# A three-stage attention kernel on one core: one masked score tile moved from TensorE to VectorE, new slot plans for its stages, and 64 extra products where two stages begin

## What is computed

```python
def stage0(q, k, mask):             # 8 heads of 16 channels, 256 positions, grouped conv (3 taps)
    qh, kh, vh = gconv(q, wq), gconv(k, wk), gconv(v, wv)
    att = softmax(qh.T @ kh / sqrt(8) - 1e9 * mask)
    return layernorm(att @ vh + q.T)
def stage1(x, mask):                # 16 heads of depth 16, 128 positions, mask shared by all
    return layernorm(x + mha(x, x, x, mask))
def stage2(x, ctx, padding):        # keys and values from ctx, a padding mask for each sequence
    return layernorm(x + mha(ctx, ctx, x, padding))
def ffn(x):
    return layernorm(x + relu(x @ w1 + b1) @ w2 + b2)
```

## Time and profile before

| | |
|---|---|
| median of 3 runs | 4481.46 us (4481.1 to 4481.8) |
| the profiled execution: its time, its span | 4476.52 us, 4474.7 us |
| PE, DVE, ACT, POOL busy, share of the span | 93%, 79%, 70%, 64% |
| mean granted TensorE clock | 0.985 |
| first stage, second, third, feed-forward begin at about | 0, 1612, 2705, 3724 us |

### The profile page before, as it was taken

One profiled execution on the slowest core, in us unless ns is written; L12 is line 12 of the kernel. 1 busy time (PEld: TensorE's weight loads), 2 busy tenths in 40 slices (PEclk: granted clock), 3 DMA queues, 4 the chain that ended last, 5 costly groups with the idle time before them and its releaser, 6 DMA issues. The chain is left out here.

```text
span 4474.7 us, 129562 instructions
## 1 busy us (share of the span) xinstructions
PE 4144.4 (93%) x46216; PEld 3376.6 (75%) x46216; DVE 3523.3 (79%) x13839; ACT 3136.7 (70%) x6279; POOL 2872.4 (64%) x4568
## 2 busy tenths in 40 slices
PE   7999999999999969999999986999999997999999
PEld 5777777777777747777777765788787776999998
DVE  7898988989988859999999985777777774555555
ACT  5777777777777748888888875777777775444443
POOL 4777777777776637777777764766766762444444
PEclk9999999999999979999999998999999998999999
DMA  5444444444444436767777756898889882222221
GB/s 137 119 125 119 123 123 120 125 120 122 122 121 123 114 94 154 169 160 172 162 165 170 162 131 144 195 197 193 194 197 193 194 184 90 71 71 71 71 71 53
DMA packets 1082953, 608.79 MB, mean 136 GB/s; under 512 B 64664, under 2 KB 1082056, under 8 KB 1082312
## 3 DMA queue, kind: packets, MB, share of 16 engines
q1 hardware_dynamic: 1071896, 595.70, 54.8%
q10 hardware_dynamic: 10416, 4.80, 0.5%
HBM read 175.66 MB, written 117.54 MB: 66 GB/s over the span
## 5 line engine op out<-in xcount | busy, mean ns | idle before, releaser
L1142 DVE CUSTOM_DVE_ANT_0 l_junk<-l_bank,mask 128x256 bf16<-128x256 f32 x2048 | 776.8, 418 | 47.6 <-PE l_bank L830 33.7
L995 ACT ACTIVATE mha_probs<-mha_bank 128x512 f32<-128x512 f32 x1024 | 611.3, 601 | 278.9 <-DVE mha_bank L1157 154.0
L995 ACT ACTIVATE l_probs<-l_bank 128x512 f32<-128x512 f32 x1024 | 604.6, 597 | 266.2 <-DVE l_bank L1157 258.8
L1157 DVE TENSOR_TENSOR l_bank<-l_bank,mask0t 128x512 f32<-128x512 f32 x768 | 530.5, 691 | 25.9 <-PE l_bank L862 22.4
L1142 DVE CUSTOM_DVE_ANT_0 mha_junk<-mha_bank,mask 128x128 bf16<-128x128 f32 x2048 | 462.3, 284 | 29.7 <-PE mha_bank L830 29.4
L830 PE MATMUL l_bank<-l_stack 96*128 96x256 bf16 x2048 | 385.2, 274 | 58.8 <-DMA l_stack<-l_parts 29.6
L830 PE MATMUL mha_bank<-mha_stack 96*128 96x128 bf16 (+1 forms) x4096 | 355.8, 221 | 79.2 <-DVE mha_max_parts L1142 48.0
L1557 ACT ACTIVATE ffn_hidden<-ffn_h,ffn_b_s 128x512 f32<-128x512 f32 x256 | 176.4, 689 | 354.8 <-PE ffn_h L1504 344.1
L862 PE MATMUL l_bank<-l_stack 99*128 99x128 bf16 x4096 | 403.1, 221 | 9.7 <-ACT l_probs L995 4.3
L1157 DVE TENSOR_TENSOR mha_bank<-mha_bank,mask1t 128x512 f32<-128x512 f32 x512 | 354.9, 693 | 71.2 <-PE mha_bank L862 66.1
L862 PE MATMUL mha_bank<-mha_stack 99*128 99x128 bf16 (+1 forms) x4096 | 395.8, 220 | 15.4 <-DMA mha_stack<-mha_max_rows 13.6
(11 more groups left out here) (197 smaller groups left out, 11430.0 us busy)
## 6 DMA issues: line engine op xcount, KB each, us to landing
mha_stack<-mha_parts SPq DMA_DIRECT2D x1536, 128.0 KB, 3.5
l_stack<-l_parts SPq DMA_DIRECT2D x1024, 64.0 KB
l_stack<-l_parts SPq DMA_DIRECT2D x256, 128.0 KB
rows_o<-mha_resid SPq DMA_DIRECT2D x64, 512.0 KB, 3.5
cols_o<-mha_y_t SPq DMA_DIRECT2D x128, 256.0 KB, 3.0
l_x_pad<-in_x SPq DMA_DIRECT2D x64, 256.0 KB, 3.3
l_c_pad<-in_ctx SPq DMA_DIRECT2D x64, 256.0 KB, 3.2
l_resid<-in_x_t SPq DMA_DIRECT2D x64, 256.0 KB, 3.2
```

The costliest lines, as they stand in the source:

```text
L995: nc.scalar.activation(probs[:, i % RING, :], tbank[i % 2][:, :], ACT.Exp).then_inc(att_exp, 1)
L1142: ins = nc.vector.tensor_tensor_reduce(out=junk[:, i % 2, cols], in0=sbank[i % 2][:, cols], in1=mask, scale=1.0, scalar=LOWEST, op0=ALU.ad ...
L1157: nc.vector.tensor_tensor(bank_, bank_, mask.unsqueeze(1).to_broadcast([P, 4, P]), ALU.add).then_inc(att_masked, 1)
```

## The change

The plans of all three stages are written anew, `pe_masks` loses step 15 (so VectorE adds that mask), and at the start of the first and the second stage TensorE multiplies the identity with itself 64 times, into a bank that is written anew before it is read. The semaphore wait for the identities now stands in the second stage too.

```diff
 PLANS = (
     dict(
-        score=[2, 3, 4, 6, 7, 8, 10, 10, 11, 12, 12, 13, 14, 14, 15, 16],
+        score=[3, 4, 5, 7, 7, 8, 10, 10, 11, 12, 12, 13, 14, 15, 16, 18],
-        pe_masks=(4, 12, 14, 15),
+        pe_masks=(4, 12, 14),
-        pool_steps={'add': (7, 0), 'power': (8, 1)},
-        work=[((0, 1), 'values', 1, 0),
+        pool_steps={'add': (7, 1), 'power': (8, 1)},
+        work=[((0,), 'values', 1, 0),
-              ((9,), 'turn_y', -1, 3),
+              ((8,), 'turn_y', -1, 3),
-              ((13,), 'turn_y', 0, 0),
+              ((12,), 'turn_y', 0, 0),
...
     dict(
-        score=[4, 4, 6, 8, 8, 9, 11, 12, 12, 13, 13, 14, 15, 15, 17, 18],
+        score=[4, 4, 7, 8, 9, 9, 11, 12, 12, 13, 13, 14, 15, 15, 17, 18],
-        pool_steps={'power': (9, 0)},
+        pool_steps={'power': (9, 2)},
-              ((5, 6), 'values', 1, 1),
+              ((5,), 'values', 1, 1),
...
     dict(
-        score=[2, 2, 4, 4, 6, 6, 8, 8, 11, 11, 12, 13, 13, 14, 15, 16],
+        score=[4, 4, 5, 7, 8, 8, 9, 9, 10, 10, 12, 13, 13, 14, 15, 18],
-        steps={'turn': 5, 'turn_merged': 7, 'output': 8, 'normalise': 9},
-        dve_steps={'recip': (5, 1), 'merge': (5, 2), 'low': (7, 1), 'add': (8, 1), 'stats': (8, 1), 'moments': (9, 0), 'epsilon': (9, 1)},
+        steps={'turn': 6, 'turn_merged': 7, 'output': 8, 'normalise': 9},
+        dve_steps={'recip': (5, 1), 'merge': (5, 1), 'low': (6, 2), 'add': (8, 2), 'stats': (8, 2), 'moments': (9, 1), 'epsilon': (9, 1)},
-        pool_steps={'power': (9, 2)},
+        pool_steps={'power': (9, 1)},
-              ((1,), 'values', 1, 1),
-              ((3,), 'max', 0, 1),
-              ((3, 4), 'project', 2, 0),
+              ((2,), 'values', 1, 1),
+              ((3,), 'project', 2, 0),
+              ((5,), 'max', 0, 1),
-              ((7,), 'turn_y', -1, 3),
+              ((9,), 'turn_y', -1, 3),
-              ((9,), 'max', 1, 0),
-              ((11,), 'project', 2, 3),
+              ((12,), 'max', 1, 0),
+              ((11, 12), 'project', 2, 3),
-        split_slot=14,
+        split_slot=13,
...
+    WARM_UP = 64
...
             if phase != 2:
                 pe.wait_ge(const_ready, 1)
-            if conv:
                 pe.wait_ge(c["pool_setup"], c["idents_ready"])
+                for n in range(WARM_UP):
+                    nc.tensor.matmul(tbank[n % 2][:, 0:P], c["identb"][:, :], c["identb"][:, :], start=True, stop=True)
```

## The result

| | before | after |
|---|---|---|
| median (4 runs each, same chip) | 4481.63 us | 4557.74 us (4555.44 to 4562.72) |
| ratio | 1 | 1.0171, 95% interval 1.0154 to 1.0189 |
| the profiled execution: its time, its span | 4476.52 us, 4474.7 us | 4562.72 us, 4560.9 us |
| PE, DVE, ACT, POOL busy | 93%, 79%, 70%, 64% | 91%, 77%, 69%, 63% |
| mean granted TensorE clock | 0.985 | 0.973 |

The change is slower, as forecast, but by 76 us where 18.5 were forecast, and 4558 us lies above the range's end at 4545.

The account below looks back on a forecast made before the run. PE's fixed order was taken as the bound, so its standing still counts. First stage -33, second 0, third +53 and 64 products -1.5 us sum to +18.5 on 4481.46: 4500 us, 8-in-10 range 4432 to 4545.

Parts of the forecast that it names:

- The path and its wait: Third stage, turn of half 1's maxima to attention step 8: path 6.1 us, cover 3.2, PE waits 2.9 a unit.
- Rival A: Third stage: maxima land in time, path under 4.4 us, stage 0 to -37 us, total 4410 to 4447; chance 0.28.
- PE then stands 6.1 - 3.2 = 2.9 us in each unit: Third stage, attention step 8: PE waits for the maxima's transfer, 2.9 us a unit, between 1.6 and 5.6.
- What the third stage gets back: Third stage: 0.48 and 0.70 us a unit returned, 1.18 in all, leaving 1.7 a unit, +53 us over 31 units.
- The 0.48 us of the turn: Third stage: turn of the heads moves from slot 5 to 6 and no longer waits for z, 0.48 us a unit.
- the 0.60 for z: Third stage: PE's wait for z stays, 0.60 us a unit, as the normalisation stands behind a merge needing a later turn.
- The 0.70 of the score steps: Third stage: scores 8 and 9 move from slot 11 to 10, so later score steps find maxima taken, 0.70 us.
- the fill wait: First stage, score step 0: PE's wait for fills of the stack goes, 0.32 us a unit, 20 us.
- the mask: First stage, step 15's mask moved to DVE: 0.2 us a unit gained, not PE's 0.55, removed products lying inside ScalarE's chain.
- rival C: First stage: DVE becomes the bound, stage gives 0, third as forecast or worse, total 4531 us and up; chance 0.12.
- rival D: Stage starts: the 64 products fail, clock at half again when inputs come, 1.5 us missing; no chance given.
- the signs that were named: Third stage: L864 waits 2 to 4 us, unit 32; first: fill wait gone, unit 23.8; second: twelve products about 2.9.

Follow-up runs that it names:

- the last experiment: Changed kernel, third stage's plan undone, score step 11 moved to slot 12 and one turn of z to the next iteration's slot 0: 4460.3 us, ratio 0.9965.

## Why the prediction was right on the sign and wrong on the size

**The path and its wait: right.** Forecast were 6.1 us against a cover of 3.2, a wait of 2.9; the stage shows a path of 6.2 and a wait of 2.8 (the view counts it from the end of the last product, 0.16 later than the cover does). The two parts of the path were an estimate of 1.1 us to the issue and 5.0 after it; they are 0.8 and 5.4, so their errors cancel in part. The experiment with half of the fills shows what sets the larger one: with the DMA engines at 1.04 to 1.20 around the transfer the step begins 5.4 us after the issue, at 0.40 to 0.76 after 3.3. Rival A rested on the transfer's own queue and on the Trainium skill's rule (DMA: Bandwidth & Descriptors, "Queues, rings and completion order") that the DMA engines go round their queues. Its price held only with the fills halved, where the wait was 0.7 us and the unit 30.7 us, as before the change (30.5); with the full traffic the trace does not bear out that a queue of its own keeps the transfer clear of SyncE's backlog. The 2.0 us of fixed time that the prediction takes from the section on the anatomy of one DMA are stated there for a transfer that GpSimd issues, and this one is ScalarE's.

**The step that failed: "PE then stands 6.1 - 3.2 = 2.9 us in each unit", as the whole price.** The sum had no term for what the pause does to PE's clock, and gave no reason for leaving it out. The clock is 1.00 in every window of the earlier trace rows of before, and I priced the wait with all other work at that speed. The run with products in the wait puts the missing term at 32 us, 1.0 a unit, and the profiles put it at 29.8 - 28.6 = 1.2 us of busy time. The Trainium skill (TensorE: Matmul & The Clock Gate, "HAM oscillation — how this bites in real kernels") describes a case of this kind, a wait for a DMA in every iteration behind which the clock is at half again; I had read the clock only for the start of the stages. The trace agrees in kind: 0.66 and 0.84 in the two windows behind the wait of the unit shown. This term alone would have made the forecast 4532 us, inside the range; the measured 4558 takes the next error too.

**"What the third stage gets back": a second term that failed.** The 0.48 us of the turn came back and the 0.60 for z stayed, both as forecast. The 0.70 of the score steps did not come back: 15.9 us in 20.7 units, 0.77. I gave it to scores 8 and 9 standing earlier. But in both plans two scores stand in slot 13 and the next in slot 14, and with score 11 in slot 12 the wait left the list: it shows at that pair, though the time did not come back with it (the last experiment). With this the account of a unit closes: 2.8 for the maxima, less 0.48, and 0.07 more for the scores, 0.04 less for z, 1.2 of clock: 3.5 us, where the unit went from 30.4 to 33.8. As totals, 99 us in place of 53: 32 are the clock, 22 (31 x 0.70) the score wait. That alone would be 107; the mean wait, 2.8 in place of 2.9, takes 3 off, and 5 stay within the spread of the runs. The new plan without its late turn of the maxima costs 12 us against that of before, so nothing else in it gains either.

**The first stage: right in sign and size, not shown in its mechanism.** Forecast -33, measured -26. The slots gave 17 us (forecast 20 for the fill wait), the mask 9 (forecast 63 x 0.2 = 13). That 17 is near 20 is in part luck: the fill wait went, as forecast, but the larger wait for ScalarE's copy of the heads came with the same slots, and the gain shows in PE's busy time, which the forecast did not touch. The mask's 0.14 us in place of PE's 0.55 agrees with the forecast that the removed products lie inside ScalarE's chain, but does not show it: the wait of 27 us for ScalarE's copy stands there with the mask kept too, and only that for its z (5.3 us) came with the mask. VectorE did not become the bound (922 of 1000 us), so rival C falls.

**The second stage and the 64 products: as forecast**, no difference that the runs can tell. The products save 2.0 us where they stand in the second stage, and nothing at the end that can be told from the spread (rival D in effect, though not by its reason: in the second stage the clock did hold until the inputs came).

**The total closes:** 18.5 forecast, 99 - 53 = 46 more in the third stage, and 34.5 - 23 = 11.5 less gained in the rest, are the 76 measured. Of the signs that were named, the wait of L864 came, and the unit was 33.8 us in place of 32; the first stage's unit was 23.95 (23.8), the twelve products 3.0 us (2.9).

## What to carry to other kernels

A wait in every iteration of a loop that TensorE bounds costs more than its length: look at the granted clock behind it, and price its work at the lower level too. Here 2.8 us of pause cost some 3.8. A small transfer with a queue of its own still pays for the bulk traffic of others, so read its time where the DMA engines are as busy as at the place to which it is moved, window by window (1.22 here before the change, in a stage whose mean is 0.89), not over the stage. And when a wait is credited to a move, first find the two instructions that make it; moved entries of a tight plan exchange one wait for another.

## What the hardware showed that I had not expected

- A pause of 2.8 us on average (longest 3.9) lowers the clock in the work behind it, and waits of 2.0 (longest 2.8) and 1.7 (longest 2.6) still do: 0.97 and 0.98 over the window. From 2900 to 3550 us the clock fell 16 times in 19 units with the first, 11 times in 20 with the second, 7 times in 20 with the third, and never with the 40 products. What decides in which unit it falls was not tried.
- Forty products that nobody needs, put in a pause that is there anyway, made the kernel some 32 us faster.
- 24 KB on a queue that carried nothing else reached the waiting step 5.4 us after the issue on average, and 3.3 with half of the fills on another queue left out. Whether it is the DMA engines or the memory behind them that the two share was not separated.
